# Splitting the second normalisation's rows into fp16 halves ahead of their store, and turning them by fp16 transposes

## The chip, the cores and the metric

The kernel runs on one core of one Trainium2 chip. The metric is the device time of one execution in microseconds (us), lower is better. The core has five engines that run their own instruction streams and meet through semaphores: TensorE (PE; its weight loads are listed apart as PEld), VectorE (DVE), ScalarE (ACT), GpSimd (POOL), and SyncE (SP), which here only issues transfers.

## The reference, cut to what matters

Four sequences of 512 tokens of width 512 pass through a gated cross attention (16 heads, 64 context rows each) and then a gated feed-forward with eight experts of which each token takes two, beside one shared expert.

```python
x = x + jnp.tanh(g_xattn[0]) * xattn(_layernorm(x), ctx_512, Wq, Wkv_expand, Wout)
x = x + jnp.tanh(g_ffn[0]) * ffn(_layernorm(x), gate_w, w1, w2, w3, ws1, ws2, ws3)

def ffn(x, ...):
    scores = softmax(xf @ gate_w.T); weights, idx = top_k(scores, 2)
    h = einsum('td,eid->eti', xf, w1)
    g = silu(h) * einsum('td,eid->eti', xf, w3)
    eo = einsum('eti,edi->etd', g, w2)
    comb = einsum('tke,tk->te', one_hot(idx, E), weights)
    y = einsum('etd,te->td', eo, comb)
    z = silu(xf @ ws1.T) * (xf @ ws3.T) @ ws2.T
    return y + z
```

The change touches the second `_layernorm(x)`: its result, called xf in the feed-forward, is used by the shared expert and the router right away, and by the routed experts later, through a table in DRAM.

## The kernel before, in words

Every fp32 factor of a product is held as two fp16 halves, `hi` (the value rounded to fp16) and `lo` (what the rounding left), and a product is three fp16 matmuls (hi·hi, hi·lo, lo·hi), made by `product`. ACT makes `hi` and DVE makes `lo` nearly everywhere.

The program has two parts. **The first part** takes the four sequences (b = 0 to 3) one after the other, in 4 tiles (i = 0 to 3) of 128 tokens. It is a software pipeline written out by hand: `iteration(b, prev, nxt)` on each engine first runs the feed-forward of sequence `prev` = b-1 (`feed_forward`, for the last one `last_feed_forward`), mixed with the rest of the attention of sequence b. b = 1 and b = 2 are one loop body, passed twice. Each engine has its own order of calls, and a call waits on semaphores only.

The place that the change touches is where the attention of a sequence f ends and its feed-forward begins. TensorE makes four tiles of attention output (`y_mm`); DVE adds each to x (`make_x1`, L858), takes its statistics (`statistics2`, L826; `aggregate2`, L833 and L837), POOL raises the variance to the power -0.5 (`power2`, L414, two tiles at a time), and DVE writes the normalised tiles `xn2` in fp32 (`norm2`, L880, two tiles at a time). `xn2` has two readers. SP stores it to the DRAM table `xrows` (`store_rows`, L332). TensorE turns it (`turn_x2`: four fp32 transposes of 128 x 128 into one PSUM bank, L1293), ACT copies the bank to the hi half of `x2T` (`turn_hi`, L536), and DVE subtracts that from the bank and writes the lo half (`turn_lo`, L810). `x2T` feeds the shared expert (`hidden`, 12 matmuls a tile) and the router. Between `turn_x2(f, 0)` and `turn_x2(f, 1)` TensorE computes the last scores of the next sequence (`scores(c, 3)`).

For the last sequence (`last_feed_forward(3)`) the engines also split the experts' weights into halves, in 16 pieces (`split_piece`): ACT makes the hi half, and DVE or POOL (L458) the lo half. The router's choices become lists of (token, weight) pairs in DRAM, which POOL scatters (L431) and SP reads back.

**The second part** has 39 tiles of 128 (token, expert) pairs. For tile j POOL gathers rows of `xrows` into one of three slots of `G` (L504); TensorE turns them by four fp32 transposes (`turn_rows`), ACT and DVE make the halves `GT` (`rows_hi`, `rows_lo`); then come 12 matmuls (`hidden_e`), the activation, 2 fp32 transposes of `gg`, 6 matmuls into `Y`, and POOL adds the rows of `Y` to `out` in DRAM (L521). TensorE turns the rows of tile j+2 while tile j is under way.

Of the kernel before, what the change touches and what calls it, by code (L numbers as in the profile page):

```python
# [32 lines left out]
P = 128  # L33
# [4 lines left out]
TOK = B * SQ  # L38
# [32 lines left out]
def block_program(nc, x, ctx_rows, gates, wq, wkv, wout, gate_w, experts, out):  # L71
    with ExitStack() as stack:  # L72
# [7 lines left out]
        xrows = nc.dram_tensor("xrows", (ROWS, D), F32)  # L80
# [53 lines left out]
        G = sb("G", [P, RING, D])  # L134
        GT = sb("GT", [P, RING, 2, DC, P], F16)

        shared_raw = [G[:, :, :].rearrange("p s d -> p (s d)"),
                      GT[:, :, :, :, :].rearrange("p s h c t -> p (s h c t)").bitcast(F32)]
        Y = sb("Y", [P, RING, D])
# [63 lines left out]
        ln2_step, ln2_stats, xn2_ready = sem("ln2_step"), sem("ln2_stats"), sem("xn2_ready")  # L203
        lg_mm, lg_max, lg_out, lg_exp = sem("lg_mm"), sem("lg_max"), sem("lg_out"), sem("lg_exp")
# [86 lines left out]

        def pass_waits(eng):


            eng.sem_inc(passed, 1)  # L295
# [6 lines left out]
        def _(sp):  # L302
# [15 lines left out]
            sp.dma_start(xrows[TOK:ROWS, :].rearrange("(n p) d -> p n d", p=P), spare).then_inc(st_init, 16)  # L318
# [66 lines left out]
        def _(pool):  # L385
# [36 lines left out]
            pool.wait_ge(consts, CONSTS)  # L422
            power1(0)
# [110 lines left out]
        def _(act):  # L534
# [48 lines left out]
            def turn_hi(b, kind, i):  # L583

                number, bank_ = turn_no(b, kind, i)
                act.wait_ge(turned, number)
                turn_halves(lambda dst, src: hi(dst[0], src), kind, i, bank_).then_inc(turned_hi, 1)
# [30 lines left out]
            def feed_forward(f, nxt):  # L618
# [46 lines left out]
            def last_feed_forward(f):  # L665

                c = f + 1
                turn_hi(c, "x2", 0)
                turn_hi(c, "x2", 1)
                split_piece(8)  # L670
# [134 lines left out]
        def _(dve):  # L805
# [69 lines left out]
            def norm2(b, p):  # L875
                if not isinstance(b, int) or b > 0:
                    dve.wait_ge(st_rows, 64 * b)
# [24 lines left out]
            def turn_lo(b, kind, i):  # L902
                number, bank_ = turn_no(b, kind, i)
                dve.wait_ge(turned_hi, number)
# [122 lines left out]

            def after_attention(f):
# [592 lines left out]
```

## Time and profile before

| | us |
|---|---|
| median of 3 runs | 525.69 (525.18 to 526.63) |
| profiled execution | 525.32 |
| its span, first to last instruction | 523.5 |
| PE busy | 435.4 (83%) |
| DVE busy | 322.2 (62%) |
| ACT busy | 246.0 (47%) |
| POOL busy | 240.2 (46%) |
| mean granted TensorE clock | 0.947 of full speed |

The span is cut by stages: the first part lasts until the first gathered rows arrive at 320.4 us, the second from there to about 514 us. "Busy" counts overlapping, pipelined matmuls once. A low share of an engine over the whole span tells nothing of a single place: what matters is which wait ends last there.

### The profile page before, as it was taken

What the parts mean: (1) busy time and instruction counts of PE and PEld (TensorE: products, weight loads), DVE (VectorE), ACT (ScalarE), POOL (GpSimd) and SP (SyncE); (2) the same over time, 40 slices, a digit from 0 to 9 for tenths busy, and PEclk for the clock granted to TensorE, in tenths of its full rate; (3) what the DMA queues carried; (4) which work ended last, traced back from release to release, by engine and by line L of the source; (5) the groups of instructions that cost most, each with busy time, mean ns of one, the idle gap of its engine ahead of it and who ended that gap; (6) DMA issues with size and microseconds to landing.
All of it is one profiled execution on the core that took longest, in us unless ns stands there. A gap on an engine that the chain in (4) does not pass through costs nothing. (4 is left out here: it accounts for less than half of the span.)

```text
span 523.5 us, 8113 instructions
## 1 busy us (share of the span) xinstructions
PE 435.4 (83%) x2432; PEld 233.2 (45%) x2433; DVE 322.2 (62%) x641; ACT 246.0 (47%) x425; POOL 240.2 (46%) x185
## 2 busy tenths in 40 slices
PE   2699699988999889987756723999999999999991
PEld 1355455554555545544323311454555455455540
DVE  4798768887588865898888952343434343434330
ACT  4877554563356534486733611333433444333430
POOL 4008235405544154466583633255455455555532
PEclk9999789999999999999895975999999999999996
DMA  8970001120011100325649554166666665756652
GB/s 310 418 307 1 0 1 41 41 81 2 1 60 42 60 0 0 117 105 180 242 121 258 131 113 112 30 108 115 120 104 104 114 120 87 123 112 104 121 75 42
DMA packets 26375, 55.31 MB, mean 106 GB/s; under 512 B 9136, under 2 KB 9264, under 8 KB 25712
## 3 DMA queue, kind: packets, MB, share of 16 engines
q0 software_dynamic: 9760, 20.49, 22.2%
q1 hardware_dynamic: 16592, 34.54, 20.3%
q8 instruction: 11, 0.18, 0.1%
q14 instruction: 12, 0.10, 0.1%
HBM read 31.51 MB, written 23.50 MB: 105 GB/s over the span
## 5 line engine op out<-in xcount | busy, mean ns | idle before, releaser
L1288 PE MATMUL bank<-arena 128*128 128x512 f16 (+1 forms) x576 | 111.0, 350 | 3.2 <-issue 1.5
L1288 PE MATMUL bank<-arena,GT 128*128 x468 | 109.2, 384 | 0.2 <-issue 0.2
L521 POOL DMA_INDIRECT out<-Y,entry x39 | 61.6, 1579 | 84.0 <-ACT Y L787 41.1
L1288 PE MATMUL bank<-arena,gT 128*128 (+1 forms) x330 | 81.3, 383 | 5.4 <-DVE gT L810 4.9
L1288 PEld LDWEIGHTS bank<-arena 128*128 128x128 f16 x576 | 56.3, 99 | 52.6 <-issue 5.8
L536 ACT ACTIVATE arena<-bank 128x512 f16<-128x512 f32 (+1 forms) x88 | 49.8, 586 | 50.9 <-PE bank L1288 31.3
L1288 PEld LDWEIGHTS bank<-arena,GT 128*128 128x128 f16 x468 | 46.3, 99 | 48.3 <-issue 2.9
L810 DVE TENSOR_TENSOR GT<-bank,GT 128x512 f16<-128x512 f32 x39 | 27.0, 692 | 61.0 <-ACT GT L536 61.0
L452 POOL TENSOR_TENSOR arena<-arena,rd 128x1024 f32<-128x1024 f32 x16 | 30.5, 1905 | 52.3 <-DVE rd L923 52.3
L1288 PEld LDWEIGHTS bank<-arena,gT 128*128 128x128 f16 x330 | 32.1, 98 | 42.3 <-DVE gT L810 4.6
L1252 DVE SCALAR_TENSOR_TENSOR uu<-th,bank 128x256 f32<-128x256 f32 x39 | 16.4, 421 | 55.8 <-ACT th L772 55.8
L504 POOL DMA_INDIRECT G<-xrows,entry x39 | 38.8, 994 | 26.1 <-issue 12.6
L1288 PE MATMUL bank<-arena,x2T 128*128 128x512 f16 x192 | 46.6, 395 | 4.4 <-DVE x2T L810 4.4
L787 ACT ACTIVATE Y<-bank,entry 128x512 f32<-128x512 f32 x39 | 26.8, 688 | 44.7 <-PE bank L1288 44.7
L772 ACT ACTIVATE th<-bank 128x256 f32<-128x256 f32 x39 | 15.0, 384 | 69.4 <-PE bank L1288 69.4
L445 POOL TENSOR_TENSOR arena<-arena,mx 128x1024 f32<-128x1024 f32 x16 | 30.3, 1899 | 26.4 <-DVE mx L912 26.4
L431 POOL DMA_INDIRECT lists<-pair,slot x32 | 34.4, 1075 | 16.7 <-issue 16.7
L1293 PE MATMUL bank<-ident,G 128*128 128x128 f32 x156 | 25.1, 285 | 20.2 <-DMA G<-xrows,entry 15.8
L1293 PE MATMUL bank<-ident,arena 128*128 128x128 f32 x192 | 30.6, 302 | 13.6 <-DVE arena L810 8.9
L810 DVE TENSOR_TENSOR arena<-bank,arena 128x512 f16<-128x512 f32 x48 | 31.5, 685 | 9.6 <-ACT arena L536 9.1
L1293 PEld LDWEIGHTS bank<-ident,arena 128*128 128x128 f32 x192 | 24.1, 154 | 23.3 <-DVE arena L810 10.0
L811 DVE SCALAR_TENSOR_TENSOR arena<-bank,arena 128x512 f16<-128x512 f32 (+1 forms) x40 | 25.7, 654 | 13.7 <-ACT arena L536 13.5
(126 smaller groups left out, 602.2 us busy)
## 6 DMA issues: line engine op xcount, KB each, us to landing
x_sb<-in_experts SPq DMA_DIRECT2D x16, 768.0 KB, 6.0
xrows<-xn SPq DMA_DIRECT2D x16, 256.0 KB, 2.1
out<-x_sb SPq DMA_DIRECT2D x16, 256.0 KB, 2.2
xrows<-Y SPq DMA_DIRECT2D x1, 2304.0 KB, 24.5
out<-Y SPq DMA_DIRECT2D x1, 2304.0 KB, 28.6
x_sb<-in_x SPq DMA_DIRECT2D x2, 1024.0 KB, 9.1
x_sb<-in_x SPq DMA_DIRECT2D x1, 2048.0 KB, 16.4
arena<-in_wq SPq DMA_DIRECT2D x1, 1024.0 KB, 9.3
```

The lines of the kernel that those rows point to most:

```text
L431: nc.gpsimd.indirect_dma_start(out=lists[:, :], out_offset=bass.IndirectOffsetOnAxis(ap=slot[:, i, k:k + 1], axis=0), in_=pair[:, i, k, :] ...
L445: nc.gpsimd.tensor_tensor(sv, sv, mx[:, i, :].unsqueeze(2).to_broadcast([P, NH, SK]), ALU.subtract).then_inc(sub_ready, 1)
L452: nc.gpsimd.tensor_tensor(sv, sv, rd[:, i, :].unsqueeze(2).to_broadcast([P, NH, SK]), ALU.mult).then_inc(p_ready, 1)
L504: nc.gpsimd.indirect_dma_start(out=G[:, j % RING, :], out_offset=None, in_=xrows[:, :], in_offset=bass.IndirectOffsetOnAxis(ap=entry[:, j, ...
L521: nc.gpsimd.indirect_dma_start(out=out, out_offset=bass.IndirectOffsetOnAxis(ap=entry[:, j, 0:1], axis=0), in_=Y[:, j % RING, :], in_offse ...
L536: return nc.scalar.activation(dst, src, ACT.Copy, scale=scale)
L787: nc.scalar.activation(Y[:, s, :], e_y[s][:, :], ACT.Copy, scale=entry[:, bass.ds(j, 1), 1:2].rearrange("p n c -> p (n c)").bitcast(F32)). ...
L810: return V.tensor_tensor(dst, src, high, ALU.subtract)
L811: return V.scalar_tensor_tensor(out=dst, in0=src, scalar=scale, in1=high, op0=ALU.mult, op1=ALU.subtract)
L1252: V.scalar_tensor_tensor(out=uu[:, s, :], in0=th[:, s, :], scalar=1.0, in1=e_h[s][:, 0:INTER], op0=ALU.add, op1=ALU.mult).then_inc(eu_read ...
L1288: last = nc.tensor.matmul(dst, a, b, start=n == 0, stop=n == len(steps) - 1)
L1293: last = nc.tensor.transpose(dst[:, c * P:(c + 1) * P], src[:, c * P:(c + 1) * P], ident[:, :])
```

## The change

The rows are split into fp16 halves before anything reads them. ACT writes the hi half of a normalised tile and DVE the lo half into a new tile `xnh` (new functions `rows_half` on both engines). SP stores those 1,024 fp16 values of a row, as many bytes as the 512 fp32 values before, and TensorE turns them by eight fp16 transposes into one bank read as fp16 (`turn_half_rows`, with an fp16 identity). What leaves the bank is then halves already: ACT copies the first half of the bank, and DVE copies the second instead of subtracting. In the second part the same is done to the gathered rows. `Y`, `G` and `xnh` share one SBUF tensor `rows`. ACT's `rows_half`, not DVE's `norm2`, now waits for the stores of the sequence before.

```diff
-        xrows = nc.dram_tensor("xrows", (ROWS, D), F32)
+        xrows = nc.dram_tensor("xrows", (ROWS, 2 * D), F16)
...
+        rows = sb("rows", [P, 2 * RING * D])
+        Y = rows[:, 0:RING * D].rearrange("p (s d) -> p s d", s=RING)
+        G = rows[:, RING * D:2 * RING * D].bitcast(F16).rearrange("p (s c) -> p s c", s=RING)
+        xnh = rows[:, 0:PER * D].bitcast(F16).rearrange("p (i h d) -> p i h d", i=PER, h=2)
+        ident16 = sb("ident16", [P, P], F16)
...
             def store_rows(b):
                 for i in range(PER):
-                    sp.wait_ge(xn2_ready, 4 * b + i + 1)
+                    sp.wait_ge(x2_lo, 4 * b + i + 1)
                     sp.dma_start(xrows[bass.ds((4 * b + i) * P, P), :],
-                                 xn2[:, i * D:(i + 1) * D]).then_inc(st_rows, 16)
+                                 xnh[:, i].rearrange("p h d -> p (h d)")).then_inc(st_rows, 16)
...
+            def rows_half(b, i):
+
+                act.wait_ge(xn2_ready, 4 * b + i + 1)
+                act.wait_ge(st_init, 48)
+                if not isinstance(b, int) or b > 0:
+                    act.wait_ge(st_rows, 64 * b)
+                hi(xnh[:, i, 0, :], xn2[:, i * D:(i + 1) * D]).then_inc(x2_hi, 1)
...
                 c = f + 1
+                rows_half(f, 0)
+                rows_half(f, 1)
+                scores_out(c, 3)
                 turn_hi(c, "x2", 0)
-                scores_out(c, 3)
                 turn_hi(c, "x2", 1)
                 exps(c, 2)
+                rows_half(f, 2)
+                rows_half(f, 3)
                 tanh_h(f, 0)
...
-                hi(GT[:, s, 0], e_turn[:, :].rearrange("p (c t) -> p c t", c=DC)).then_inc(eT_hi, 1)
+                hi(GT[:, s, 0], halves(e_turn, 0)).then_inc(eT_hi, 1)
...
+            def rows_half(b, i):
+
+                dve.wait_ge(x2_hi, 4 * b + i + 1)
+                lo(xnh[:, i, 1, :], xn2[:, i * D:(i + 1) * D], xnh[:, i, 0, :]).then_inc(x2_lo, 1)
...
                 if not isinstance(f, int) or f < B - 1:
-                    turn_lo(c, "x2", 0)
+                    rows_half(f, 0)
                 statistics2(f, 3)
                 aggregate2(f, 1)
+                rows_half(f, 1)
+                norm2(f, 1)
+                turn_lo(c, "x2", 0)
                 turn_lo(c, "x2", 1)
-                norm2(f, 1)
...
-                lo(GT[:, s, 1], e_turn[:, :].rearrange("p (c t) -> p c t", c=DC), GT[:, s, 0]).then_inc(eT_lo, 1)
+                V.tensor_copy(GT[:, s, 1], halves(e_turn, 1)).then_inc(eT_lo, 1)
...
+            def turn_half_rows(dst, src):
+                for c in range(2 * DC):
+                    last = nc.tensor.transpose(dst[:, :].bitcast(F16)[:, c * P:(c + 1) * P],
+                                               src[:, c * P:(c + 1) * P], ident16[:, :])
+                return last
...
             def turn_x2(f, i):
-                pe.wait_ge(xn2_ready, 4 * f + i + 1)
+                pe.wait_ge(x2_lo, 4 * f + i + 1)
                 turn_tile(f + 1, "x2", i)
```

`last_feed_forward` has the same calls: on ACT `rows_half` 0 and 1, `turn_hi` 0 and 1, `rows_half` 2 and 3, and only then `split_piece(8)`; on DVE `rows_half(3, 0)` stands ahead of `make_x1(3, 3)`, where `turn_lo` of tile 0 stood.

On DVE, at the loop's head (the last `make_x1` of the attention stands ahead of the branch), the order was this before; `xn` is `xn2`, `bank` a PSUM bank, `mx` the head maxima:

```order
L858 SCALAR_TENSOR_TENSOR x_sb<-bank,gl,x_sb 128x512 [waits y_mm]
L1240 UNCONDITIONAL_BRANCH
L1240 ISA
L810 TENSOR_TENSOR x2T<-bank,x2T 128x4x128 [waits turned_hi]
...
L826 BN_STATS mv<-x_sb 128x6
...
L837 TENSOR_SCALAR ln<-ln 128x2 [waits ln2_step]
...
L810 TENSOR_TENSOR x2T<-bank,x2T 128x4x128 [waits turned_hi]
...
L880 TENSOR_SCALAR xn<-x_sb,ln 128x512 x2
L911 ISA
L912 TENSOR_REDUCE mx<-arena 128x16 [waits s_copied]
```

And this is the order of the changed kernel at the same place, where `rows` holds `xnh` and L839 is DVE's new `rows_half`:

```order
L887 SCALAR_TENSOR_TENSOR x_sb<-bank,gl,x_sb 128x512 [waits y_mm]
L1282 UNCONDITIONAL_BRANCH
L1282 ISA
L839 TENSOR_TENSOR rows<-xn,rows 128x512 [waits x2_hi]
...
L855 BN_STATS mv<-x_sb 128x6
...
L839 TENSOR_TENSOR rows<-xn,rows 128x512 [waits x2_hi]
...
L907 TENSOR_SCALAR xn<-x_sb,ln 128x512 x2
L932 ISA
L933 COPY x2T<-bank 128x4x128 [waits turned_hi]
...
L933 COPY x2T<-bank 128x4x128 [waits turned_hi]
L839 TENSOR_TENSOR rows<-xn,rows 128x512 [waits x2_hi] x2
L942 ISA
L943 TENSOR_REDUCE mx<-arena 128x16 [waits s_copied]
```

Four instructions `rows_half` are added, and the copies of tiles 0 and 1 out of the bank moved behind both `norm2` instructions.

TensorE's order at the same place in the changed kernel (L1340 is `turn_half_rows`, 128x256 are the last scores, and the matmuls on `x2T` are `hidden(f, 0)`):

```order
L1372 ISA [waits x2_lo]
L1340 MATMUL bank<-ident,rows 128x128 [waits turned_lo]
L1340 MATMUL bank<-ident,rows 128x128 x7
L1433 ISA
L1330 MATMUL bank<-arena 128x256 [waits s_copied]
L1330 MATMUL bank<-arena 128x256 x5
L1330 MATMUL bank<-arena 128x256 [waits s_copied]
L1330 MATMUL bank<-arena 128x256 x5
...
L1340 MATMUL bank<-ident,rows 128x128 [waits turned_lo]
L1340 MATMUL bank<-ident,rows 128x128 x7
...
L1330 MATMUL bank<-arena,x2T 128x512 [waits turned_lo]
```

Nothing moved on TensorE: four transposes became eight, and they wait for `x2_lo`, DVE's `rows_half`, where they waited for `xn2_ready`.

## Rows read from the trace of the kernel before

**Rows 1.** Windows: busy (instructions) of PE, PEld, DVE, ACT, POOL; clock; DMA; GB/s.

```profile
80.00:240.00 160.00, 146.30 (x952) 83.13 (x950) 127.88 (x258) 84.39 (x149) 72.70 (x50) 1.00 0.14 50
338.30:514.00 175.70, 168.70 (x872) 87.38 (x870) 67.81 (x146) 68.06 (x146) 92.20 (x71) 1.00 0.63 107
273.30:287.00 13.70, 8.65 (x69) 4.87 (x70) 11.99 (x23) 4.17 (x5) 5.36 (x3) 0.50 0.83 221
```

**Rows 2.** Timeline of PE in the second part: start, us, instruction, [idle before].

```profile
334.42 0.60 PE L1293 MATMUL bank<-ident,G 128*128 128x128 f32 x4
334.86 0.38 PE L1293 MATMUL bank<-ident,gg 128*128 128x128 f32 x2
...
338.96 0.60 PE L1293 MATMUL bank<-ident,G 128*128 128x128 f32 x4
```

**Rows 3.** Timeline of PE where sequence 1's feed-forward begins.

```profile
149.40 0.60 PE L1293 MATMUL bank<-ident,xn 128*128 128x128 f32 x4
149.83 1.47 PE L1288 MATMUL bank<-arena 128*128 128x256 f16 x12
151.14 0.60 PE L1293 MATMUL bank<-ident,xn 128*128 128x128 f32 x4
152.78 2.76 PE L1288 MATMUL bank<-arena,x2T 128*128 128x512 f16 x12 [1.04 <-DVE x2T L810]
156.49 2.75 PE L1288 MATMUL bank<-arena,x2T 128*128 128x512 f16 x12
159.30 0.75 PE L1288 MATMUL bank<-gate_s,x2T 128*128 128x8 f16 x24
159.90 2.75 PE L1288 MATMUL bank<-arena,x2T 128*128 128x512 f16 x12
```

**Rows 4.** Timeline of DVE at the same place.

```profile
151.40 0.73 DVE L858 SCALAR_TENSOR_TENSOR x_sb<-bank,gl,x_sb 128x512 f32 x1
152.05 0.68 DVE L810 TENSOR_TENSOR x2T<-bank,x2T 128x512 f16<-128x512 f32 x1
153.75 0.17 DVE L837 TENSOR_SCALAR ln<-ln 128x2 f32<-128x2 f32 x1
153.85 0.69 DVE L810 TENSOR_TENSOR x2T<-bank,x2T 128x512 f16<-128x512 f32 x1
154.87 1.00 DVE L880 TENSOR_SCALAR xn<-x_sb,ln 128x512 f32 x2 [0.33 <-POOL ln L414]
```

**Rows 5.** Timelines of POOL and ACT at the same place.

```profile
154.00 0.70 POOL L414 TENSOR_TENSOR ln<-ln,minus_half 128x2 f32<-128x2 f32 x1 [2.04 <-DVE ln L837]
148.14 1.06 ACT L598 ACTIVATE arena<-arena 128x1024 f32<-128x1024 f32 x1 [2.04 <-POOL arena L445]
150.69 1.25 ACT L593 ACTIVATE arena<-bank 128x512 f32<-128x512 f32 x2
```

**Rows 6.** Groups by line: 128x512 from SBUF to SBUF, ACT and DVE.

```profile
L536 ACT ACTIVATE ctx_s<-arena 128x512 f16<-128x512 f32 x1 | 0.6, 629 | 2.7 <-DMA arena<-in_wkv 2.7
L811 DVE SCALAR_TENSOR_TENSOR ctx_s<-arena,ctx_s x1: 692/692/692, 6.4 to 6.4; 128x512 f16<-128x512 f32 x1
```

**Rows 7.** Weight loads by line: busy, mean ns of one.

```profile
L1288 PEld LDWEIGHTS bank<-arena,GT 128*128 128x128 f16 x468 | 46.3, 99 | 48.3 <-issue 2.9
```

**Rows 8.** Timeline where the last feed-forward begins.

```profile
268.06 2.76 PE L1288 MATMUL bank<-arena,x2T 128*128 128x512 f16 x12 [1.44 <-DVE x2T L810]
274.32 1.12 PE L1293 MATMUL bank<-ident,xn 128*128 128x128 f32 x4 [3.50 <-DVE xn L880]
270.89 6.32 POOL L458 TENSOR_TENSOR arena<-x_sb,arena 128x1536 f16<-128x1536 f32 x2
271.02 6.47 DVE L880 TENSOR_SCALAR xn<-x_sb,ln 128x512 f32<-128x512 f32 x2 [0.33 <-POOL ln L414]
281.20 0.80 PE L1288 MATMUL bank<-gate_s,x2T 128*128 128x8 f16 x24 [1.92 <-DVE x2T L810]
```

More of the change, by code:

```diff
@@ L203, in block_program @@
         ln2_step, ln2_stats, xn2_ready = sem("ln2_step"), sem("ln2_stats"), sem("xn2_ready")
+        x2_hi, x2_lo = sem("x2_hi"), sem("x2_lo")
         lg_mm, lg_max, lg_out, lg_exp = sem("lg_mm"), sem("lg_max"), sem("lg_out"), sem("lg_exp")
@@ L290, in turn_halves, with halves @@
             return make(dst, src)
+        def halves(bank_, h):
+            return bank_[:, :].bitcast(F16)[:, h * D:(h + 1) * D].rearrange("p (c t) -> p c t", c=DC)
         def pass_waits(eng):
@@ L317, in _ @@
             spare = Y[:, 0:1, :].to_broadcast([P, (ROWS - TOK) // P, D])
-            sp.dma_start(xrows[TOK:ROWS, :].rearrange("(n p) d -> p n d", p=P), spare).then_inc(st_init, 16)
+            spare16 = rows[:, 0:D].bitcast(F16).unsqueeze(1).to_broadcast([P, (ROWS - TOK) // P, 2 * D])
+            sp.dma_start(xrows[TOK:ROWS, :].rearrange("(n p) d -> p n d", p=P), spare16).then_inc(st_init, 16)
             sp.dma_start(out[TOK:ROWS, :].rearrange("(n p) d -> p n d", p=P), spare).then_inc(st_init, 16)
@@ L422, in _ @@
             pool.wait_ge(consts, CONSTS)
+            nc.gpsimd.tensor_copy(ident16[:, :], ident[:, :]).then_inc(consts, 1)
             power1(0)
@@ L586, in turn_hi @@
                 act.wait_ge(turned, number)
+                if kind == "x2":
+                    hi(x2T[:, 0, :, i * P:(i + 1) * P], halves(bank_, 0)).then_inc(turned_hi, 1)
+                    return
                 turn_halves(lambda dst, src: hi(dst[0], src), kind, i, bank_).then_inc(turned_hi, 1)
@@ L667, in last_feed_forward @@
                 c = f + 1
+                rows_half(f, 0)
+                rows_half(f, 1)
                 turn_hi(c, "x2", 0)
                 turn_hi(c, "x2", 1)
+                rows_half(f, 2)
+                rows_half(f, 3)
                 split_piece(8)
@@ L903, in turn_lo @@
                 number, bank_ = turn_no(b, kind, i)
+                if kind == "x2":
+                    dve.wait_ge(turned_hi, number)
+                    V.tensor_copy(x2T[:, 1, :, i * P:(i + 1) * P], halves(bank_, 1)).then_inc(turned_lo, 1)
+                    return
                 dve.wait_ge(turned_hi, number)
@@ L1031, in after_attention @@
                 if not isinstance(f, int) or f < B - 1:
[L1032 removed]
+                    rows_half(f, 0)
                 statistics2(f, 3)
                 aggregate2(f, 1)
+                rows_half(f, 1)
+                norm2(f, 1)
+                turn_lo(c, "x2", 0)
                 turn_lo(c, "x2", 1)
[L1036 removed]
             def feed_forward(f, nxt):
@@ L1046, in feed_forward @@
                 after_attention(f)
+                rows_half(f, 2)
+                rows_half(f, 3)
                 head_max(c, 3)
@@ L1127, in last_feed_forward @@
                 after_attention(f)
+                rows_half(f, 2)
+                rows_half(f, 3)
                 split_piece(7)
@@ L1213, in iteration @@
                 if not nxt:
-                    turn_lo(b + 1, "x2", 0)
+                    rows_half(b, 0)
                 make_x1(b, 3)
@@ L1324, in turn_tile @@
                     pe.wait_ge(turned_lo, number - 2)
-                src = {"x": xn1, "x2": xn2, "p": S, "g": gg[:, i % 2, :]}[kind]
+                if kind == "x2":
+                    turn_half_rows(bank_, xnh[:, i].rearrange("p h d -> p (h d)")).then_inc(turned, 1)
+                    return
+                src = {"x": xn1, "p": S, "g": gg[:, i % 2, :]}[kind]
                 n = IC if kind == "g" else DC
@@ L1539, in turn_rows @@
                     pe.wait_ge(eT_lo, j)
-                turn(e_turn, G[:, s, :], DC).then_inc(eT_mm, 1)
+                turn_half_rows(e_turn, G[:, s, :]).then_inc(eT_mm, 1)
             def hidden_e(j, s, e):
```

7 lines of the change are left out of this document (2 added, 5 removed).

## The prediction

> **What bounds the kernel now.** I read the windows first: in the middle of the second part PE is busy 168.7 of 175.7 us at full clock, in the loop of the first part 146.3 of 160.0 us, while DVE is busy 127.9 of those 160 [rows 1]. The second part is PE's; its other engines have more than half of their time free (DVE 67.8 of 175.7). The first part is PE's too, but DVE has little to spare, and PE's missing 14 us are waits on it. So I read PE's own timeline next, tile by tile.
>
> In the second part a tile takes 4.54 us (from 334.42 to 338.96), and the four fp32 transposes of the gathered rows take 0.44 us of it (334.42 to 334.86) [rows 2]. There is no wait in that stretch. Whatever DVE saves there saves nothing; only PE's own time counts.
>
> In the first part the place to read is the head of a feed-forward. At 149.40, right behind the attention's last output product, PE turns `xn2` tile 0 with no wait, then makes 12 score matmuls, turns tile 1 at 151.14, and waits 1.04 us for DVE's `turn_lo` before the first `hidden` at 152.78 [rows 3]. DVE meanwhile runs with hardly a gap: `make_x1(3)` at 151.40, `turn_lo` of tile 0 at 152.05, statistics, variance at 153.75, `turn_lo` of tile 1, and `norm2` of tiles 2 and 3 at 154.87 [rows 4]. So for some 4 us DVE is what ends last here. The same rows stand 62.5 us earlier and later, at the heads of sequences 0 and 2.
>
> **The change, part by part.**
>
> *Eight fp16 transposes for four fp32.* Each of the eight streams 128 fp16 columns. The nearest row by dtype and weight load is the score group: 12 fp16 matmuls of 256 columns, each with its own weight load, from 149.83 to 151.14, so 0.109 us each and 0.055 for 128 columns [rows 3]. Eight are 0.44 us, what the four took. From below: 24 router matmuls of 8 columns, each with a load, fill 159.30 to 159.90, so 0.025 us each [rows 3]; eight would be 0.20, a gain of 0.24 a tile. From above: if no load hid behind a stream, 0.099 each [rows 7], eight are 0.79, a loss of 0.35 a tile. I take 0.055, since the loads are of the same kind as those of the score group and the router shows that they fit in 0.025. So the second part changes by 0, between 39 x -0.24 = -9.4 and 39 x +0.35 = +13.7 us; with the 16 tiles of the first part -13.2 and +19.3.
>
> The Trainium skill speaks against this on the page "TensorE: Matmul & The Clock Gate", section "Back-to-back issue gap": in a stream of weight load and matmul pairs it gives about 81 ns for one of 128 columns. By that figure eight would take 0.65 us and the second part would grow by some 8 us, an estimate from the page. The score row does not show such a surcharge, and no row here has 128 fp16 columns.
>
> *The second part's DVE and ACT.* ACT copies 512 columns from a bank as before. DVE's subtraction becomes a copy, which can only be shorter; DVE is half idle there [rows 1]: 0. The gathers move as many bytes per row: 0.
>
> *The heads of feed-forwards 0, 1 and 2.* I redo sequence 1's head on its own times. ACT's `rows_half` of tile 0 and 1 cost 0.63 each [rows 6]; ACT is free at 149.20 [rows 5], so both are done by 150.5, hidden behind DVE, which is not ready. DVE's `rows_half(0)` cannot start before `make_x1(3)` has left, at 152.05, and reads two SBUF operands for 512 columns: 0.69 [rows 6]. So `x2_lo` comes at 152.75 and PE turns tile 0 at about 152.8, not at 149.40. Queued behind that wait on PE is everything: the scores, which had no need of `xn2` (152.8 + 0.44 + 1.31 = 154.55). DVE: variance at 153.75 as before, `rows_half(1)` 153.85 to 154.55, so tile 1 is turned at 154.6. POOL's power had started at 154.00 and taken 0.70 [rows 5]; I let it wait until `rows_half(1)` is over (below), 154.55 to 155.25. `norm2` starts 0.17 us later as before, at 155.4, and takes 0.92 until the next can start, 156.35. Then `turn_lo` of tile 0, a copy out of a bank: between 0.5 (half of the `norm2` pair) and 0.68 (the subtraction) [rows 4]; I take 0.55. `hidden(f, 0)` starts at 156.9, before at 152.78: +4.1. ACT is not later: scores copied by 155.4 (1.25 for two [rows 5]), then two `turn_hi`.
>
> Late next are tiles 2 and 3: ACT's `turn_hi(1)` ends at 156.5, `exps` 1.06 [rows 5] at 157.5, two `rows_half` at 158.6; DVE follows to 159.3. `hidden(f, 0)` streams until 159.5, so this is just hidden (0.2 of cover; without it a few tenths). `hidden(f, 1)` starts at about 160.5, before at 156.49 [rows 3]: **+4.0**. DVE itself runs 3.4 late by then (four `rows_half` 2.7, longer power 0.55, less on the copies), so it does not add to PE's shift. All that follows moves along, and PE has no slack to take it back. Three heads: **+12.0**. If the copies are 0.68, the power is not held and so on, a head is between +3.3 and +4.6: 9.9 to 13.8.
>
> The hold on the port: DVE's `norm2` of 1.00 us for two took 6.47 us when it met POOL's 6.32 us of `split_piece` [rows 8]. The Trainium skill, page "SBUF — State Buffer", section "Terms", says why: the port pair that DVE and GpSimd share is locked exclusively and the loser waits for the whole instruction. The old `turn_lo` read a bank and `x2T`, the new `rows_half` reads two SBUF tiles, so it can hold POOL and be held; by a rule that left `rows_half` free of this a head would cost 3.5 instead of 4.0. The trace agrees for `norm2`; for a subtraction of two SBUF tiles my rows don't settle it.
>
> *The clock.* Between 149.4 and 152.8 PE will idle 3.4 us, and about 1.9 more before `hidden(f, 0)`. At 270.8 it idled 3.50 us, and from 273.3 the granted clock was 0.50, the lower level of 1.2 GHz, for 13.7 us [rows 1, 8]. If it falls at a head, the turn and the scores take 1.75 us more, of which some 1.5 reach `hidden`. I take this for half of the heads: **+2.3**, between 0 and 3 x 4 = 12 (a `hidden` of 2.6 us at half clock too).
>
> *The head of feed-forward 3.* PE's turns of tiles 0 and 1 wait for DVE's `rows_half`, which stands before and after `make_x1(3, 3)`, and `hidden(3, 0)`, at 268.06 before, now waits for `turn_lo(0)` behind `norm2`. But `norm2` was held until 277.5 by two POOL pieces [rows 8], and the second of these is piece 8, whose hi half ACT now makes only after `rows_half(3, 3)`. So `norm2` is held by one piece, 3.2 us, and ends near 275.4. Then `turn_lo` twice, `hidden(3, 0)` at 276 (2.6 us at full clock, 5.2 at half), turns, halves, and the second router group, at 281.20 before: 280.5 to 283.7. The list of choices, its scatter and the gather hang on it: -1 to +3, I take **+1**. `ident16` on POOL is hidden behind loads at the start: 0.
>
> *Sum.* 525.3 (the profiled execution: span 523.5 and 1.8 around it) + 12.0 + 2.3 + 1 + 0 = 540.6. The median is 525.7, 0.4 above; I give **540.8**.
>
> **The rivals.** *(A) As summed*, heads +10 to +20 in all: 535 to 546. Chance 0.70.
> *(B) The weight loads show in the transposes*: towards 0.099 each, +19 at the bound, so 546 to 560. For it: no fp16 transpose is in the trace. Against: 0.025 for a load and 8 columns [rows 3]. The skill's 81 ns falls under it. Chance 0.10.
> *(C) The clock falls at every head and stays*: +24 in all, about 551. For it: 13.7 us of it at 273.3 [rows 1]. Chance 0.10.
> *(D) The shift is taken back*: PE waits for DVE elsewhere in the loop too (14 us in 160 [rows 1]), and if those waits belong to fixed times of ACT or POOL, the later start falls into them: 526 to 528. Against: DVE is 3.4 us late itself. The change shows nothing then. Chance 0.05.
> *(E) Faster: the fp16 transposes are cheaper than any row.* PE turns 55 tiles; against +15.3 that needs more than 0.28 us saved a tile, so under 0.020 us for a transpose, less than the router's matmuls of 8 columns take [rows 3]. At nothing at all it would be 525.7 + 15.3 - 24 = 517. Chance 0.05.
>
> **How the numbers follow.** The time is that of (A). The range reaches from below the low end of (A), with heads at 3.3 and no fall of the clock (525.7 + 9.9 - 1 = 534.6, less 1 for the halves' copies), to (C): 533 to 551, which leaves out part of (B), (D) and (E). A measurement of this kernel tells 0.3%, 1.6 us, from no change. Slower: A, B, C and half of D; faster: E; the same: the rest.
>
> **What would show it.** Right: the first `hidden` starts 7.5 us after the attention's last product has been issued (149.40 before), instead of 3.4; PE waits about 3 us for `rows` ahead of the turn of tile 0 in three heads; in the second part a tile still takes 4.54 us and eight transposes 0.44; `norm2` of the last sequence ends some 2 us earlier. Wrong: a tile of another length in the second part (B or E), no PE wait ahead of the turn, or a wait that ends on ACT.

## The result and the profile after

The changed kernel takes 544.83 us (median of 4 runs, 540.07 to 545.5) against 526.16 us (525.18 to 527.62) for the kernel before: a ratio of 1.033, 95% interval 1.027 to 1.040. It is 18.7 us slower; 540.8 with 533 to 551 was forecast. Ratios here and below leave out runs more than 1.5% above the fastest of their kernel, which matters for the last kernel below (four of its 13), and a ratio isn't quite the quotient of the medians. The profiled execution has a span of 543.1 us, 19.6 more than before, and a mean granted clock of 0.930 instead of 0.947.

Windows of the changed kernel (columns as in [rows 1]). The first line is the loop of the first part, the second the second part; the last four are stretches whose granted clock is the lower of its two levels, 1.2 GHz: one at each of the heads of sequences 0, 1 and 2, and the one at the last head.

```profile
80.00:240.00 160.00, 139.26 (x907) 78.55 (x906) 119.14 (x241) 77.27 (x141) 61.45 (x44) 0.96 0.12 43
354.00:534.00 180.00, 172.99 (x1039) 88.85 (x1037) 59.82 (x150) 69.80 (x150) 94.22 (x73) 1.00 0.62 105
91.70:95.20 3.50, 3.50 (x25) 2.75 (x22) 2.16 (x7) 1.14 (x3) 1.10 (x1) 0.51 0.42 151
160.00:163.40 3.40, 2.79 (x18) 1.98 (x16) 1.88 (x4) 2.02 (x4) 1.10 (x1) 0.50 0.35 130
228.30:235.10 6.80, 6.02 (x24) 2.88 (x22) 4.83 (x8) 4.13 (x7) 1.19 (x2) 0.50 0.29 109
282.90:296.50 13.60, 6.33 (x27) 3.05 (x28) 11.39 (x16) 5.64 (x8) 8.33 (x7) 0.50 0.67 156
```

In this window PE was busy 146.3 of the 160 us before, at a clock of 1.00 [rows 1], and is now busy 139.3 at 0.96. The second part stays PE's. Most of the loss is in the first part.

Timeline of PE in the second part, one tile (beside [rows 2]), and the group of the copy that DVE makes there:

```profile
410.89 0.61 PE L1340 MATMUL bank<-ident,rows 128*128 128x128 f16 x8
411.33 0.39 PE L1335 MATMUL bank<-ident,gg 128*128 128x128 f32 x2
...
415.45 0.61 PE L1340 MATMUL bank<-ident,rows 128*128 128x128 f16 x8
```

```profile
L1290 DVE COPY GT<-bank 128x512 f16<-128x512 f16 x39 | 16.6, 425 | 59.8 <-ACT GT L546 59.8
```

Eight fp16 transposes take 0.44 us, as four fp32 ones did, and a tile 4.56 us (4.54 before). DVE needs 0.425 instead of 0.69 us for its half, and waits longer for ACT.

Timeline of PE at the head of sequence 1 (beside [rows 3]), then of DVE, POOL and ACT there (beside [rows 4, 5]):

```profile
159.14 0.61 PE L1340 MATMUL bank<-ident,rows 128*128 128x128 f16 x8 [3.56 <-DVE rows L839]
159.59 2.35 PE L1330 MATMUL bank<-arena 128*128 128x256 f16 x12
161.74 1.06 PE L1340 MATMUL bank<-ident,rows 128*128 128x128 f16 x8
163.58 2.76 PE L1330 MATMUL bank<-arena,x2T 128*128 128x512 f16 x12 [0.78 <-DVE x2T L933]
```

```profile
157.42 0.73 DVE L887 SCALAR_TENSOR_TENSOR x_sb<-bank,gl,x_sb 128x512 f32 x1
158.07 0.68 DVE L839 TENSOR_TENSOR rows<-xn,rows 128x512 f16<-128x512 f32 x1
...
159.88 0.69 DVE L839 TENSOR_TENSOR rows<-xn,rows 128x512 f16<-128x512 f32 x1
161.28 1.00 DVE L907 TENSOR_SCALAR xn<-x_sb,ln 128x512 f32 x2 [0.71 <-POOL ln L423]
163.09 0.92 DVE L933 COPY x2T<-bank 128x512 f16<-128x512 f16 x2 [0.81 <-ACT x2T L546]
160.03 1.10 POOL L423 TENSOR_TENSOR ln<-ln,minus_half 128x2 f32<-128x2 f32 x1 [2.05 <-DVE ln L866]
155.13 1.13 ACT L546 ACTIVATE rows<-xn 128x512 f16<-128x512 f32 x2
```

This is the predicted chain: ACT's halves are early (done by 156.3), DVE writes the lo half only behind `make_x1`, PE waits 3.56 us, the power is held, then `norm2`, then the copies, then `hidden`. One thing differs: the 12 score matmuls take from 159.59 to 161.74, 2.15 us instead of 1.31, since the clock fell at 160.0. ACT copies the scores ahead of tile 0's hi half, so DVE's copies then wait 0.81 us for ACT.

I measure a head from the start of the last matmul of the attention's output ("the last product") to the start of `hidden(f, 1)`, for the sequences 0, 1 and 2 in this order, here and for every kernel below, in its profiled execution. The last head is the same stretch of sequence 3. Where the start of `hidden(f, 0)` is meant, the text says so.

| kernel | median, us | ratio to before | to `hidden(f, 1)`: 0, 1, 2 | last head |
|---|---|---|---|---|
| before | 526.16 | 1 | 7.15, 7.31, 7.55 | 17.78 |
| changed | 544.83 | 1.033 | 11.92, 11.86, 13.14 | 20.13 |

So the three heads are 4.8, 4.6 and 5.6 us longer, 14.9 together, and the last one 2.3. The rest of the 19.6 us of span has both signs. There are 1.3 us ahead of the first head, which the change doesn't explain: the kernel before with its two waits masked (`b0_control` below) also reaches it at 87.7 us. There are 1.1 in one idle gap of PE in the loop that the trace puts to no engine. Between head 2 and the last head 1.7 us are taken back, 1.3 of them where PE waits for `mask`, the router's choices, which DVE makes. Before, a DVE instruction on 128x32 ahead of `mask` took 3.12 us instead of 0.19, beside a piece of 3.10 us on POOL that started at 245.31; now that the heads are later the piece starts just behind that instruction, and the wait shrinks (the kernel before, then the changed one):

```profile
251.05 0.19 PE L1361 MATMUL bank<-mask,earlier 128*128 128x32 f16 x1 [1.99 <-DVE mask L971]
268.32 0.19 PE L1412 MATMUL bank<-mask,earlier 128*128 128x32 f16 x1 [0.68 <-DVE mask L1002]
```

Behind the last head come 1.7 more: the first gathered rows are turned 61.4 us behind the last product of sequence 3 instead of 56.4, and the second part is 1.1 us shorter. Not all of this belongs to the change: in `b0_control` the rows come after 58.1, and in the five kernels below that have the changed last head after 57.1 to 61.4.

### The profile page after: what moved, and what is told of

It reads as the page before. It is cut to its first block and busy times, and to the rows that moved or that the text cites. A ratio compares the mean times of both kernels' runs of the same rounds, so it can differ in the third digit from the quotient of the medians.

```text
span 543.1 us, 8598 instructions
## 1 busy us (share of the span) xinstructions
PE 443.6 (82%) x2652; PEld 235.9 (43%) x2653; DVE 314.7 (58%) x657; ACT 253.6 (47%) x441; POOL 241.4 (44%) x186
## 5 line engine op out<-in xcount | busy, mean ns | idle before, releaser
L1330 PE MATMUL bank<-arena 128*128 128x512 f16 (+1 forms) x576 | 113.6, 356 | 4.3 <-issue 2.7
L531 POOL DMA_INDIRECT out<-rows,entry x39 | 61.6, 1579 | 83.3 <-ACT rows L816 38.9
L1330 PE MATMUL bank<-arena,gT 128*128 (+1 forms) x330 | 83.2, 390 | 5.5 <-DVE gT L839 5.0
L1340 PE MATMUL bank<-ident,rows 128*128 128x128 f16 x440 | 36.0, 231 | 35.9 <-DVE rows L839 16.3
L1330 PE MATMUL bank<-arena,x2T 128*128 128x512 f16 x192 | 49.7, 414 | 6.1 <-DVE x2T L933 6.1
L1340 PEld LDWEIGHTS bank<-ident,rows 128*128 128x128 f16 x440 | 29.8, 103 | 52.5 <-issue 33.5
L514 POOL DMA_INDIRECT rows<-xrows,entry x39 | 38.7, 993 | 28.7 <-DMA entry<-lists 14.7
L1290 DVE COPY GT<-bank 128x512 f16<-128x512 f16 x39 | 16.6, 425 | 59.8 <-ACT GT L546 59.8
L816 ACT ACTIVATE rows<-bank,entry 128x512 f32<-128x512 f32 x39 | 26.8, 688 | 44.7 <-PE bank L1330 39.0
L839 DVE TENSOR_TENSOR arena<-bank,arena 128x512 f16<-128x512 f32 x48 | 31.4, 685 | 10.1 <-ACT arena L546 9.8
```

The lines of the kernel that those rows point to most:

```text
L514: nc.gpsimd.indirect_dma_start(out=G[:, j % RING, :], out_offset=None, in_=xrows[:, :], in_offset=bass.IndirectOffsetOnAxis(ap=entry[:, j, ...
L531: nc.gpsimd.indirect_dma_start(out=out, out_offset=bass.IndirectOffsetOnAxis(ap=entry[:, j, 0:1], axis=0), in_=Y[:, j % RING, :], in_offse ...
L816: nc.scalar.activation(Y[:, s, :], e_y[s][:, :], ACT.Copy, scale=entry[:, bass.ds(j, 1), 1:2].rearrange("p n c -> p (n c)").bitcast(F32)). ...
L839: return V.tensor_tensor(dst, src, high, ALU.subtract)
L1330: last = nc.tensor.matmul(dst, a, b, start=n == 0, stop=n == len(steps) - 1)
L1340: last = nc.tensor.transpose(dst[:, :].bitcast(F16)[:, c * P:(c + 1) * P], src[:, c * P:(c + 1) * P], ident16[:, :])
```

## The experiments

In all of them, the yardstick `a0_after` included, the register values in two waits (POOL's for the landed list entries, PE's for the split pieces) are masked to their low bits. Line numbers shift by a few between the kernels.

The first four were timed together, beside 523.55 us (520.09 to 527.5, 7 runs) for the kernel before.

**The changed kernel with the masks.**

> The changed kernel; only the two register values that TensorE and GpSimd wait against in the second part are masked to small positive numbers. Both theories: 540 to 546 us, as the changed kernel (544.8). It is the yardstick for the kernels beside it.

Measured: 537.88 us (537.61 to 540.28), ratio 1.028 (1.022 to 1.034). Heads 14.25, 12.06 and 10.96, last head 19.68. The interval overlaps with that of the changed kernel; the heads already show that they differ from one sequence to the next within one execution. Heads 0 and 1 had a stretch of lower clock, head 2 had none: 10.96 is what this head takes at full clock.

**The heads alone.** The rows are stored and gathered in fp32, and the second part is that of before.

```diff
-                    sp.wait_ge(x2_lo, 4 * b + i + 1)
+                    sp.wait_ge(xn2_ready, 4 * b + i + 1)
...
-                hi(GT[:, s, 0], halves(e_turn, 0)).then_inc(eT_hi, 1)
+                hi(GT[:, s, 0], e_turn[:, :].rearrange("p (c t) -> p c t", c=DC)).then_inc(eT_hi, 1)
...
-                turn_half_rows(e_turn, G[:, s, :]).then_inc(eT_mm, 1)
+                turn(e_turn, G[:, s, :], DC).then_inc(eT_mm, 1)
```

> The heads of the feed-forwards stay as changed (halves first, fp16 turns, waits on DVE's half), but the table, the gathered rows and the second part are fp32 as before. Theory that all of the loss is in the first part: 540 to 546, as the changed kernel, and a tile of the second part still 4.5 us. Rival that the fp16 gather and turns cost in the second part: 526 to 535.

Measured: 539.43 us (536.58 to 540.93), ratio 1.029 (1.022 to 1.036); heads 12.04, 11.86, 14.21. The whole loss without the second part's edit.

**The second part alone.** The heads turn fp32 rows in the order of before; the halves are made for the store only, where DVE and ACT have room.

```diff
-                    rows_half(f, 0)
+                    turn_lo(c, "x2", 0)
...
+                if prev is not None:
+                    for i in range(PER):
+                        rows_half(prev, i)
```

> The other half alone: the heads turn xn2 in fp32 as before, the halves are made later (behind the probabilities; in the last feed-forward behind the second tanh) for the store alone, and the second part gathers and turns fp16. Theory that the loss is PE's wait for the halves at the heads: 525 to 530, although ACT and DVE still make all 16 tiles of halves. Rival that the extra work of DVE (16 x 0.69 us) or the fp16 rows cost wherever they are: 536 to 545.

Measured: 525.81 us (524.2 to 527.33), ratio 1.004 (0.998 to 1.010); heads 7.14, 7.31, 7.10, last head 16.70. The same 16 pairs of halves, the fp16 store, the fp16 gathers and all 312 fp16 transposes of the second part are in it, and no loss that the timing can tell, which leaves room for 5 us. The power takes 0.70 us in the three heads. This refutes the rival of the weight loads, and says that most of the cost comes from the place of the halves, not from their work. In one place the work does show: the four halves of sequence 2 on DVE, 2.50 us together, stand ahead of `mask` in the last iteration, and PE waits 4.40 us for it instead of 1.99; the last head, 1.1 us shorter, gives half of that back.

**PE kept busy while it waits.** Fourteen matmuls of 512 columns, whose result nobody reads, ahead of the turn of tile 0.

```diff
+                pe.wait_ge(turned_lo, turn_no(c, "x2", 0)[0] - 2)
+                for _ in range(14):
+                    nc.tensor.matmul(turn_no(c, "x2", 0)[1][:, :], earlier[:, :], wkv_s[:, 0, 0:D],
+                                     start=True, stop=True)
                 turn_x2(f, 0)
```

> The changed kernel; in the heads of feed-forwards 0, 1 and 2 TensorE makes 14 matmuls of 512 columns that nothing reads, ahead of its wait for tile 0, some 3.0 us. Theory that the fall of the clock at each head costs about 1 us (0 to 2) beside the wait: the clock stays full at the three heads, hidden(f,0) starts 0.8 to 1.8 us earlier after the last attention product, and the time is 3 to 5 us below the changed kernel. Rival that only DVE's chain sets the head: clock full, time within 1 us of the changed kernel.

Measured: 534.87 us (533.24 to 537.23), ratio 1.021 (1.015 to 1.027), 3.0 us under the median of `a0_after`; the times of the two kernels don't overlap. Timeline of PE at the head of sequence 1, and a window over the head:

```profile
152.91 3.19 PE L1460 MATMUL bank<-wkv_s,earlier 128*128 128x512 f16 x14
156.29 0.62 PE L1340 MATMUL bank<-ident,rows 128*128 128x128 f16 x8 [0.20 <-DVE rows L839]
156.74 1.47 PE L1330 MATMUL bank<-arena 128*128 128x256 f16 x12
158.18 0.62 PE L1340 MATMUL bank<-ident,rows 128*128 128x128 f16 x8
160.15 2.76 PE L1330 MATMUL bank<-arena,x2T 128*128 128x512 f16 x12 [1.35 <-DVE x2T L933]
```

```profile
152.90:166.40 13.50, 11.95 (x85) 6.72 (x84) 10.32 (x21) 6.46 (x12) 4.90 (x3) 1.00 0.21 78
```

The clock is 1.00, the scores take 1.44 us again, and the heads are 10.81, 10.96 and 10.95 against 7.15, 7.31 and 7.55 before: +3.7, +3.7 and +3.4, 10.7 us in all. That is what the halves and the new order cost at full clock. There `hidden(f, 0)` starts 7.32, 7.46 and 7.46 us after the last product started. The heads of `a0_after` are 4.5 us longer in all than these, and the times differ by 3.0: `a0_after` waits only 0.56 us for `mask`, this kernel 1.99, as before, which accounts for 1.4 us between the two figures.

The next four were timed beside 525.95 us (523.35 to 528.66, 7 runs).

**The scores ahead of the turn.** They do not need the rows.

```diff
-                turn_x2(f, 0)
                 scores(c, 3)
+                turn_x2(f, 0)
                 turn_x2(f, 1)
```

> The changed kernel; on TensorE scores(c, 3) stands ahead of turn_x2(f, 0) instead of behind it (heads 0, 1, 2). Theory that DVE's chain (halves, power, norm2, copy) sets hidden(f,0) and the queue order on PE only decides whether the clock falls: PE's hole shrinks to 2.2 us, the clock stays full, and from the last attention product to hidden(f,1) it is 10.9 to 11.1 us as in the filled kernel, so the time is as the filled kernel's, 2 to 4 us below the changed one (ratio to before 1.018 to 1.024). Rival that the scores queued behind the wait are themselves the loss: 1.3 us less a head again, ratio 1.010 to 1.015.

Measured: 543.73 us (541.6 to 546.05), ratio 1.035 (1.027 to 1.042). I had expected the clock to stay full. Timeline of PE at head 1, and its stretch of lower clock there:

```profile
156.75 0.66 PE L1340 MATMUL bank<-ident,rows 128*128 128x128 f16 x8 [1.98 <-DVE rows L839]
158.56 1.03 PE L1340 MATMUL bank<-ident,rows 128*128 128x128 f16 x8 [1.16 <-DVE rows L839]
160.53 4.46 PE L1330 MATMUL bank<-arena,x2T 128*128 128x512 f16 x12 [0.94 <-DVE x2T L933]
```

```profile
157.20:164.00 6.80, 4.70 (x20) 2.03 (x18) 5.00 (x12) 3.17 (x5) 1.10 (x1) 0.50 0.29 108
```

`hidden(f, 0)` starts 7.32, 7.46 and 8.15 us behind the last product, in heads 0 and 1 exactly as in the filled kernel, so at full clock the scores behind the wait cost nothing: DVE is what it waits for either way. In the changed kernel it started 8.43, 8.37 and 7.64 us behind; in its heads 0 and 1 the scores at half clock did cost about 1 us, through ACT. But the idle time is now cut into 1.98, 1.16 and 0.94 us with little work between, the clock fell in all three heads, and it fell over `hidden(f, 0)`, 4.46 us instead of 2.76 at head 1. The heads are 12.36, 12.65 and 13.20.

**The turns twice in the second part**, as a price of the transposes measured by itself.

```diff
+                turn_half_rows(e_turn, G[:, s, :])
                 turn_half_rows(e_turn, G[:, s, :]).then_inc(eT_mm, 1)
```

> The changed kernel; the eight fp16 transposes of each of the 39 tiles of the second part are made twice. Theory that the second part is TensorE's and a transpose costs 0.055 us: a tile takes 4.97 to 5.0 us instead of 4.55, 39 x 0.44 = 17 us more than the changed kernel (ratio to before 1.055 to 1.068). Rival that a transpose waits for its weight load (0.099): 31 us more. Rival that the second part waits on something else: under 5 us more.

Measured: 551.6 us (551.37 to 554.61), ratio 1.050 (1.043 to 1.058). Timeline of PE, one tile, and a window over the second part, of this kernel and then of `a0_after`:

```profile
435.75 1.06 PE L1340 MATMUL bank<-ident,rows 128*128 128x128 f16 x16
436.64 0.39 PE L1335 MATMUL bank<-ident,gg 128*128 128x128 f32 x2
...
440.75 1.06 PE L1340 MATMUL bank<-ident,rows 128*128 128x128 f16 x16
```

```profile
341.53:538.17 196.64, 194.77 (x1373) 110.14 (x1372) 62.18 (x155) 74.04 (x154) 94.38 (x73) 1.00 0.56 97
```

```profile
338.65:524.45 185.80, 180.44 (x1076) 92.72 (x1076) 62.02 (x155) 71.20 (x154) 94.27 (x73) 0.99 0.58 104
```

Sixteen take 0.89 us and the tile 5.00, so eight more cost 0.44, 0.055 us each, as measured for the first eight. But the second part grew by 10.8 us, not by the 17 (39 x 0.44) that I expected. In `a0_after` 11 tiles take 4.7 to 5.1 us instead of 4.56, 4.8 us more in all, with waits of PE ahead of the turns, which the trace puts to the gathered rows or to nothing that it shows. With the turns twice every tile from the fourth on takes 5.00, so the longer turns fill what had been waits. The turns of tiles 0 and 1 lie ahead of the two windows, which is 0.9 us more, and 0.7 stay open. The ratio was expected at 1.055 at least and came out lower for this reason.

**PE doesn't wait for the halves.** It turns fp32 rows with no wait, as before; DVE and ACT keep the changed order.

```diff
             def turn_x2(f, i):
-                pe.wait_ge(x2_lo, 4 * f + i + 1)
+                pe.wait_ge(xn2_ready, 4 * f + i + 1)
                 turn_tile(f + 1, "x2", i)
```

> The changed kernel, but TensorE turns xn2 in fp32 as soon as it is ready, as before, and ACT and DVE make x2T as before; the halves are still made at the same places of ACT's and DVE's changed order, for the store. So PE waits for no half. Theory that DVE's order (two halves and norm2 ahead of tile 0's turn_lo) sets the head: from the last attention product to hidden(f,1) still 10.9 to 12 us, time within 2 us of the changed kernel with a full clock (ratio 1.018 to 1.028). Rival that PE's wait for x2_lo is the loss: 8 us or less, ratio under 1.010.

Measured: 543.03 us (540.62 to 543.73), ratio 1.032 (1.025 to 1.039). Timeline of PE at head 1:

```profile
153.65 0.60 PE L1328 MATMUL bank<-ident,xn 128*128 128x128 f32 x4
154.08 1.47 PE L1323 MATMUL bank<-arena 128*128 128x256 f16 x12
155.39 0.60 PE L1328 MATMUL bank<-ident,xn 128*128 128x128 f32 x4
161.16 4.80 PE L1323 MATMUL bank<-arena,x2T 128*128 128x512 f16 x12 [5.17 <-DVE x2T L836]
```

The 3.56 us in front of the turn are gone and stand, as 5.17 us, in front of `hidden(1, 0)`, which starts 7.73 us behind the last product, in the filled kernel 7.46. The 0.27 between them is DVE's: it subtracts here, 0.68 us, where the other copies, 0.42. The heads are 13.52, 13.25 and 13.15 and not the 10.9 to 12 that I expected with a full clock: the clock fell behind the wait here too, over `hidden(f, 0)` (4.80 us at head 1). The wait that the change adds on PE is where the loss shows, and is not its cause.

**Reordered.** The copy of tile 0 ahead of `norm2`, the scores ahead of the turn, and ACT's halves of tiles 2 and 3 ahead of `exps`.

```diff
                 rows_half(f, 1)
-                norm2(f, 1)
                 turn_lo(c, "x2", 0)
+                norm2(f, 1)
                 turn_lo(c, "x2", 1)
```

> The changed kernel in another order: scores ahead of the turn of tile 0 on TensorE, tile 0's copy ahead of norm2 on DVE, the halves of tiles 2 and 3 ahead of the exponential on ACT. Theory that DVE's chain sets the head: hidden(f,0) comes 1.5 to 2.5 us earlier than in the filled kernel, hidden(f,1) 0.5 to 1.5 us (10.9 to 9.4 to 10.4 from the last attention product), ratio to before 1.013 to 1.020. Rival that something else ends last (ACT, or the power on POOL): as the kernel with the scores first.

Measured: 536.43 us (535.76 to 538.17), ratio 1.021 (1.014 to 1.028). Timeline of DVE at head 1:

```profile
155.50 0.69 DVE L839 TENSOR_TENSOR rows<-xn,rows 128x512 f16<-128x512 f32 x1
156.10 0.42 DVE L933 COPY x2T<-bank 128x512 f16<-128x512 f16 x1
156.90 1.00 DVE L907 TENSOR_SCALAR xn<-x_sb,ln 128x512 f32 x2 [0.37 <-POOL ln L423]
```

`hidden(f, 0)` starts 5.81, 6.31 and 6.77 us behind the last product, so DVE's order moves it, by 1.2 to 1.5 us against the scores ahead of the turn alone; I had expected 1.5 to 2.5 against the filled kernel, and it is 0.7 to 1.5. The copy is short enough to fit into the time in which DVE waits for the power. What ends last now is `rows_half` of tile 1: PE turns that tile 5.49 us behind the last product at head 1, and `hidden(1, 0)` follows with no wait. The clock fell in all three heads and took part of the gain away (10.96, 12.14, 12.82 to `hidden(f, 1)`, where 9.4 to 10.4 was expected); the last head is 16.95, 0.8 shorter than before the change. ACT's order was changed too, so this run doesn't show the swap on DVE by itself beyond `hidden(f, 0)`.

The last three were timed together, beside 526.32 us (522.85 to 530.83, 29 runs).

**The kernel before with the masks.**

> The kernel before with the two register values of waits masked to their low bits, as every experiment here has them. Expected by every theory: the kernel before's time, ratio 0.997 to 1.003, heads of 7.2 to 7.6 us from the last output product to the second hidden. If it is outside 0.3%, the masks cost something and the yardstick of all experiments moves by as much.

Measured: 527.39 us (524.35 to 529.19), ratio 1.000 (0.997 to 1.003). The masks cost nothing. Its profiled execution has the heads of before (7.14, 7.32, 7.55, 17.85) and a span that is 3.9 us longer, in stretches between the heads. So spans of single executions tell a few us only where the place of the difference is seen, and that holds for the few us outside the heads above too.

**The kernel before with PE kept busy** at the last head and while it waits for the first gathered rows (15, 10 and 64 matmuls as above).

```diff
                 hidden(f, 0)
+                pe.wait_ge(s_copied, 8 * B)
+                fill(score_bank[1], 15)
                 turn_x2(f, 2)
+                fill(score_bank[1], 10)
                 turn_x2(f, 3)
...
             pe.wait_ge(table_ready, 1)
+            fill(score_bank[1], 64)
             turn_rows(0, 0, 0)
```

> The kernel before, with PE kept busy by matmuls whose result nobody reads: 15 and 10 of 512 columns between the turns of the last feed-forward, and 64 (13.6 us at full clock) while PE waits for the first gathered rows. If what these places cost is the lower clock behind the idle time: the granted clock stays at full from 273 us on and at 320 to 328, the first two turns of the second part take 0.44 instead of 1.09 and 1.08 and the first tile 4.5 us, so 2 to 4 us come off at the second part's start and 0 to 2 at the last head: ratio 0.990 to 0.997. Rival: the places are bounded by DVE, POOL and the gathers, and the clock costs nothing there: ratio 0.998 to 1.002. Other rival: the matmuls are in the way of the real ones and it is 1 to 3 us slower.

Measured: 525.83 us (523.1 to 530.05), ratio 0.999 (0.995 to 1.003). Timeline of PE at the start of the second part, and of `b0_control` at the same place:

```profile
308.61 13.98 PE L1298 MATMUL bank<-wkv_s,earlier 128*128 128x512 f16 x64
323.94 0.66 PE L1293 MATMUL bank<-ident,G 128*128 128x128 f32 x4 [1.35 <-DMA G<-xrows,entry]
326.10 0.63 PE L1293 MATMUL bank<-ident,G 128*128 128x128 f32 x4 [1.50 <-DVE GT L810]
327.36 4.31 PE L1288 MATMUL bank<-arena,GT 128*128 x12 [0.62 <-issue]
```

```profile
324.91 1.09 PE L1293 MATMUL bank<-ident,G 128*128 128x128 f32 x4 [15.97 <-DMA G<-xrows,entry]
327.50 1.08 PE L1293 MATMUL bank<-ident,G 128*128 128x128 f32 x4 [1.50 <-DVE GT L810]
328.79 1.46 PE L1288 MATMUL bank<-arena,GT 128*128 x3 [0.20 <-issue]
```

The last head is 17.78 against 17.85: nothing there, though the clock still fell in it, at 282.7, for 6.9 us instead of 13.7. DVE and POOL bound it. The turns at the second part's start take 0.66 instead of 1.09, and the first expert's product comes 0.5 us sooner behind the first turn. The two spans differ by 2.3 us, but the timing can't tell the kernel from before. I found no version that beats the kernel before.

**Reordered, and PE kept busy** at all four heads and at the second part's start: the two kernels above together, with 9 matmuls ahead of the turn of tile 0.

```diff
                 scores(c, 3)
+                pe.wait_ge(turned_lo, turn_no(c, "x2", 0)[0] - 2)
+                fill(turn_no(c, "x2", 0)[1], 9)
                 turn_x2(f, 0)
```

> The reordered version of the change (tile 0's copy ahead of norm2, scores ahead of the turn, ACT's halves ahead of exps), with the same idle matmuls at the last feed-forward and at the second part's start, and 9 more ahead of the turn of tile 0 in the three heads. If the loss is DVE's order plus the clock, as the runs so far say: the clock is full in all three heads, from the last output product to the second hidden 9.5 to 10.3 us (10.96 to 12.82 without the fills, 7.3 before), three heads +7 instead of +13 us, the last head +1, and the second part's start gives 3 back: 527 to 532, ratio 1.005 to 1.015. Rival: the two halves of each tile on DVE (2.7 us a head) can't be hidden by any order and the fills bring nothing more: ratio 1.018 to 1.024 as without them.

Measured: 531.93 us (528.18 to 541.33), ratio 1.008 (1.004 to 1.012). The profiled execution took 541.3 us, far above the median, so I read only the heads in it. Timeline of PE at head 1:

```profile
154.87 2.11 PE L1346 MATMUL bank<-wkv_s,earlier 128*128 128x512 f16 x9
156.94 0.62 PE L1340 MATMUL bank<-ident,rows 128*128 128x128 f16 x8
158.84 0.62 PE L1340 MATMUL bank<-ident,rows 128*128 128x128 f16 x8 [1.28 <-DVE rows L839]
159.29 2.75 PE L1330 MATMUL bank<-arena,x2T 128*128 128x512 f16 x12
```

The clock is full at the three heads, and they are 9.28, 9.44 and 9.95, 6.7 us above before in all: more than half of the loss in them (14.9) is gone, as expected. Against the filled kernel, also at full clock, they are 1.5, 1.5 and 1.0 us shorter, which is what the three swaps give together. The last head is 20.75 with the 15 and 10 matmuls in it, 16.95 without: in this order the rows of tiles 2 and 3 are ready before them, and they are in the way.

## Why the prediction was right, point by point

- **The bound, and the transposes at 0.** Right: 0.44 us for eight, 4.56 us a tile, and no measurable loss with the second part alone (1.004, 0.998 to 1.010). The price taken from the score group, 0.055 us for 128 fp16 columns, is what two measurements give, eight and sixteen in a row. The figure of 81 ns in the Trainium skill ("TensorE: Matmul & The Clock Gate", section "Back-to-back issue gap") is not what happens here: the measured 55 ns decides. The loads of 0.10 us each do overlap.
- **The heads, +4.0 each.** The mechanism was right, each link of it in the rows; the size is 3.6 at full clock (10.7 for three against 12.0), inside the 3.3 to 4.6 given. The sign named for it, the first `hidden` 7.5 us behind the issue of the last product, came out at 8.2, 8.2 and 7.4, and at 7.1 to 7.2 in the filled kernel. The power was held, as chosen: 1.07 to 1.11 us where it had been 0.70, in each of the heads with `rows_half` beside it, and 0.70 with the second part alone, where none stands there. That agrees with the Trainium skill ("SBUF — State Buffer", section "SBUF: two separate sides"), which counts a DVE operation with two SBUF inputs among those that hold the shared port against a GpSimd operation that reads SBUF. The copies came out shorter than my 0.55: 0.42 each, and 0.75 for two where ACT didn't keep the second waiting.
- **"Queued behind that wait on PE is everything: the scores."** Right as a description, but at full clock it carries no time: with the scores ahead of the turn `hidden(f, 0)` starts no sooner than in the filled kernel (7.32 and 7.46 us in heads 0 and 1 of both), and without the wait it starts 0.27 later. The sum had gone by DVE's times, so it was not harmed. Only with the clock down does the queue cost: the scores then take 2.15 us.
- **The clock, +2.3.** The step that was mis-sized. I let it fall in half of the heads at 1.5 us. In the four kernels with this order of PE and no fill (changed, `a0_after`, the heads alone, the turns twice) it fell in 10 of 12 heads, and these were 1.0 to 3.3 us longer than the 10.9 of a head at full clock, 1.8 on the mean. That makes 4.5 us for three heads, and 4.2 (14.9 less 10.7) in the changed kernel; the fill takes 4.5 off the heads of `a0_after` and 3.0 off the time.
- **The last head, +1.** +2.3 in the profiled execution and +1.1 to +2.3 in five others with this last head, inside -1 to +3, if it is read at `hidden(3, 1)`. Read where the first gathered rows are turned it is 5.0 in this execution, 3.4 against `b0_control`, and varies by as much from one kernel to the next. Its timeline:

```profile
288.03 3.08 POOL L468 TENSOR_TENSOR arena<-x_sb,arena 128x1536 f16<-128x1536 f32 x1
288.07 3.77 DVE L907 TENSOR_SCALAR xn<-x_sb,ln 128x512 f32<-128x512 f32 x2 [0.62 <-POOL ln L423]
292.24 4.87 PE L1330 MATMUL bank<-arena,x2T 128*128 128x512 f16 x12 [3.69 <-DVE x2T L933]
```

  `norm2` was held by one of POOL's pieces, 3.77 us instead of 6.47 [rows 8], as I had it; it ends 1.2 us earlier behind the last product, not 2. `hidden(3, 0)` now starts 12.6 us behind it (my 276 meant 11.9), before 4.0, and at half clock it takes 4.87 us. The waits of 3.50, 2.11 and 1.92 us that stood behind it before have shrunk to one of 0.61, so that 2.3 of loss are left.
- **The sum.** 12.0 + 2.3 + 1 = 15.3 was predicted, the parts measured are 10.7 + 4.2 + 2.3 = 17.2, and the ratio says 14 to 21. The heads were 1.3 too high, the clock 1.9 and the last head 1.3 too low, so the errors hid one another in part. The sum had no term for the 1.7 us that are taken back ahead of the last head, nor for the 1.3, 1.1 and 1.7 outside the heads; that no more than 2.4 is left of these four is luck.
- **The rivals.** Weight loads that show: refuted. Cheaper transposes: refuted, 0.44 for eight. The shift taken back: refuted as a whole, since nothing is taken back from one head to the next, but 1.7 us of it are ahead of the last head, at `mask` above all, in the way that the rival named. A clock that falls at each head and stays: half true, it fell at nearly all, but came back before the head was over or soon behind it, so 1.8 us each and not 4.

What stays open: why the clock fell in some heads and not in others with the same idle time, and the few us between the last head and the first gathered rows. A last head with the halves moved elsewhere, in a kernel that keeps fp16 rows and beats before, wasn't tried.

## What to carry to other kernels

An extra pass over data is free or costly by where it stands: here 16 pairs of halves cost nothing that the timing could tell when they stood elsewhere, and 10.7 us at full clock with 12 of them at the three places where DVE is what ends last; another order there brought this to 6.7. Price such an edit on the engine that ends last there, not on the engine whose wait becomes visible: taking that wait away gave nothing, and moving one copy forward on the late engine brought `hidden(f, 0)` 1.2 to 1.5 us sooner in each head. And where an edit opens a gap on PE, add the price of the clock behind the gap for nearly every occurrence, not for half of them: gaps of 3.1 to 3.6 us had it in 10 of 12 heads. And look beyond the place of the change: an edit that shifts the engines against one another moved a meeting of POOL and DVE that cost 1.3 us before.

## What the runs showed of the hardware that I had not expected

- Idle time of the same length on PE led to a lower clock in one execution and not in another: behind a wait of 3.22 us at the head of sequence 2 it fell in the changed kernel and did not in `a0_after`; behind 3.14 us at the head of sequence 0 it fell in the changed kernel, and not in the one with the turns twice. And a shorter wait is no protection: in the two kernels with the scores ahead of the turn, whose waits at head 1 are 1.98 and 1.16 or 1.20 us with eight transposes between them, it fell in all six heads.
- Matmuls that nobody reads kept the clock at 1.00 in all six heads in which they stood ahead of the turn, and cost nothing there, since DVE was what ended the wait.
- An fp16 copy of 512 columns out of a bank takes 0.425 us on DVE, the subtraction that it replaces 0.69.
- Beside a POOL piece of 3.10 us a DVE instruction on 128x32 values took 3.12 us instead of 0.19, and this wait set when TensorE could start.
